# A second feed-forward worked in pairs of steps over two blocks, with split weights shared by both, rank-2 additions in four row groups, and a2 sums on VectorE

## The reference

```python
def qlora(x, wq, A, B):                 # wq is a quarter as wide as x
    return x @ tile(wq, (1, 4)).T + (x @ A.T @ B.T) * 0.5
gate = silu(qlora(x, w1q, a1, b1))      # x: 2048 x 1024, hidden: 2752
up = qlora(x, w3q, a3, b3)
y = qlora(gate * up, w2q, a2, b2)       # a2: 2 x 2752, b2: 1024 x 2
out = layernorm(x + y)
```

## Time and profile before

| | |
|---|---|
| median of 3 runs (2038.76 to 2041.78) | 2039.27 us |
| the profiled execution: its own time, its span | 2040.68 us, 2038.9 us |
| busy over the span: PE, DVE, ACT, POOL | 1999.7, 1109.3, 798.6, 1085.7 us |
| chain that ended last | PE 73%, POOL 8%, issue 8%, DVE 5%, ACT 4%, DMA 1% |
| subtractions h2l (L577), 128x512 and 112x512 | 88, 121.9 us, mean 1386 ns |
| subtractions w13l (L489) | 96, 123.5 us, mean 1291 ns |
| products h (L1198) | 88, 60.8 us, mean 691 ns |

### The profile page before, as it was taken

The page is one execution under the profiler, slowest core; times in us unless marked ns, Lnnn a source line. Parts: engine busy times, 40 slices in busy tenths (PEclk is TensorE's granted clock), DMA queues, the critical chain, the costliest instruction groups (busy, mean ns, idle before and its releaser), DMA issues.

```text
span 2038.9 us, 26001 instructions
## 1 busy us (share of the span) xinstructions
PE 1999.7 (98%) x9472; PEld 1636.0 (80%) x9472; DVE 1109.3 (54%) x1650; ACT 798.6 (39%) x1336; POOL 1085.7 (53%) x828
## 2 busy tenths in 40 slices
PE   8999999999999999999999999999979999999998
PEld 6887878888888888888888888888857777777776
DVE  0148975689863248976432888650145353454543
ACT  3356434562333347232333742422425325153251
POOL 6446874445546444644644455445738447175381
PEclk9999999999999999999999999999989999999999
DMA  4333433233434332443433243334422405124031
GB/s 139 96 92 94 130 92 88 86 132 99 135 87 127 98 94 93 136 133 93 124 98 93 89 139 99 129 100 149 142 73 93 144 21 175 42 92 145 21 134 42
DMA packets 104173, 213.40 MB, mean 105 GB/s; under 512 B 11896, under 2 KB 18040, under 8 KB 103012
## 3 DMA queue, kind: packets, MB, share of 16 engines
q1 hardware_dynamic: 99440, 194.97, 31.1%
q10 hardware_dynamic: 4608, 16.78, 2.1%
HBM read 194.93 MB, written 16.78 MB: 104 GB/s over the span
## 4 chain that ended last, share of the span: by engine, by line
PE 73%; issue 8%; POOL 8%; DVE 5%; ACT 4%; DMA 1%; SPq 0%; POOLq 0%; DVEq 0%; ACTq 0%
PE bank L1278 23%; PE bank L1279 23%; PE bank L1280 23%; POOL w13l L489 3%; POOL h2l L577 3%; ACT junka L669 2%; PE bank L1316 2%; POOL wl L489 1%; DMA w_in_place<-in_wd 1%; PE bank L1471 1%; PE bank L1433 1%; POOL xTl L489 1%; DVE scr L961 1%; ACT wh L620 1%; POOL hql L583 1%
## 5 line engine op out<-in xcount | busy, mean ns | idle before, releaser
L489 POOL TENSOR_TENSOR wl<-w_in_place,wh 128x512 fp32r<-128x512 f32 (+2 forms) x528 | 711.1, 1350 | 663.2 <-ACT wh L620 662.7
L620 ACT CAST wh<-w_in_place 128x512 fp32r<-128x512 f32 (+2 forms) x528 | 322.4, 613 | 768.3 <-DMA w_in_place<-in_wu 287.0
L1278 PE MATMUL bank<-wh,xTh 128*128 128x512 f32 (+1 forms) x1536 | 571.9, 372 | 12.1 <-POOL wl L489 11.7
L1280 PE MATMUL bank<-wh,xTl 128*128 128x512 f32 (+1 forms) x1536 | 569.4, 371 | 0.0
L1279 PE MATMUL bank<-wl,xTh 128*128 128x512 f32 (+1 forms) x1536 | 569.3, 371 | 0.0
L1278 PEld LDWEIGHTS bank<-wh,xTh 128*128 128x128 f32 x1536 | 290.1, 189 | 63.8 <-issue 8.5
L1280 PEld LDWEIGHTS bank<-wh,xTl 128*128 128x128 f32 x1536 | 290.0, 189 | 50.4
L1279 PEld LDWEIGHTS bank<-wl,xTh 128*128 128x128 f32 x1536 | 290.1, 189 | 49.5
L1278 PE MATMUL bank<-wh,hTh 128*128 128x512 f32 (+1 forms) x704 | 274.6, 390 | 1.5 <-POOL wl L489 1.2
L1279 PE MATMUL bank<-wl,hTh 128*128 128x512 f32 (+1 forms) x704 | 274.1, 389 | 0.0
L1280 PE MATMUL bank<-wh,hTl 128*128 128x512 f32 (+1 forms) x704 | 273.9, 389 | 0.0
(11 more groups left out here) (132 smaller groups left out, 2463.2 us busy)
## 6 DMA issues: line engine op xcount, KB each, us to landing
w_in_place<-in_wg SPq DMA_DIRECT2D x160, 256.0 KB, 2.6
w_in_place<-in_wu SPq DMA_DIRECT2D x160, 256.0 KB, 2.6
w_in_place<-in_wd SPq DMA_DIRECT2D x160, 256.0 KB, 2.6
w_in_place<-in_w SPq DMA_DIRECT2D x90, 256.0 KB, 3.8
x_in_place<-in_xT SPq DMA_DIRECT2D x32, 256.0 KB, 3.6
y<-in_xtok SPq DMA_DIRECT2D x4, 2048.0 KB, 8.9
x<-y ACTq DMA_DIRECT2D x16, 512.0 KB, 4.2
xa<-x SPq DMA_DIRECT2D x16, 512.0 KB, 5.5
```

Source lines behind the costliest of these rows:

```text
L489: nc.gpsimd.tensor_tensor(lo, landed, hi.bitcast(F32), ALU.subtract).then_inc(done, 1)
L620: nc.scalar.copy(hi, piece).then_inc(hi_done, 1)
L1278: nc.tensor.matmul(dst, ah, bh, start=start, stop=False)
L1280: return nc.tensor.matmul(dst, al, bh, start=False, stop=stop)
```

## The change

The second feed-forward is worked in two halves of two blocks. Within a half, the order is by pairs p of steps (11), and for each pair both blocks bb:

- w13 comes in pieces that hold two steps, two a pair (gate, up), and is loaded, cast and subtracted once per pair and half, for both blocks. The ring is two pairs deep.
- Gate and up of both steps use four banks, and alternating pairs all eight. The four rank additions follow the 24 matmuls with w13, each on 6 rows that start at partition 0, 32, 64 or 96. For this b13, a13s and the low-rank x (`lx`) hold the three parts of the split at six rows in each row group; a13s is 102 columns wide. `low_rank_x` is three passes over 102 rows.
- The products with a2 leave TensorE: VectorE multiplies each h2 by the two a2 columns and adds (`acc`), four operations a pair. At the end of a block the sum is split (`split_sums`) and added over the partitions by four matmuls with a matrix of ones in chosen columns, `sel` (`low_rank_h`), placed after the first 18 matmuls of the output stage. h2 is not split any more.
- x of blocks 0 and 1 is turned and folded ahead of the first half; that of blocks 2 and 3 in the output stages of blocks 0 and 1. x1T has two slots.
- The norm of a block now follows its output stage tile by tile. The fills for the split (`split_b`, `split_x`, `sel`) are made by GpSimd at piece 4 of the last down stage, one after another, and b1, b3, b2 are loaded by 18 DMAs at piece 9.

```diff
+UP = 32
+QUAD = (0, UP, 2 * UP, 3 * UP)
+LX = QUAD[-1] + 3 * R
+PAIRS = STEPS // 2
...
 # sync
-                if d == 23:
+                if d == 9:
                     load_b()
...
+            def load_13(h, p):
+                n = PAIRS * h + p
+                if n >= 2:
+                    sp.wait_ge(w13_used, n - 1)
...
 # gpsimd, at piece 4
+                    nc.gpsimd.memset(braw[:, :], 0.0).then_inc(b_zero, 1)
+                    nc.gpsimd.memset(b2raw[0:LR, :], 0.0).then_inc(b_zero, 1)
+                    for part, new, old, n in ((split_b, (LORA, -1.0), (0.0, 1.0), 2 * R), (split_x, (1.0, -1.0), (0.0, 1.0), R)):
+                        for i in range(2):
+                            fill(part[:, i:i + 1], old[i])
+                            for p0 in QUAD:
+                                fill(part[p0:p0 + n + R, i:i + 1], new[i])
+                                fill(part[p0:p0 + n, i:i + 1], old[i])
...
+            def pairs(h):
+                for p in range(PAIRS):
+                    if p < PAIRS - 1:
+                        low_13(h, p + 1)
...
+                    for bb in range(2):
+                        if ends(p):
+                            low_q(h, p // 2, bb)
...
 # scalar
+                        for i in range(2):
+                            act.wait_ge(gg_done, 2 * s + i + 1)
+                            if s:
+                                act.wait_ge(h_done, 2 * s + i - 1)
+                            nc.scalar.activation(sg[0:rows, i, :], banks[4 * (s % 2) + 2 * i][0:rows, :], ACT.Silu)\
+                                .then_inc(s_done, 1)
...
 # vector
+            def pair(h, p, bb):
...
+                for i in range(2):
+                    dve.wait_ge(uu_done, 2 * s + i + 1)
+                    dve.wait_ge(s_done, 2 * s + i + 1)
+                    V.tensor_tensor(h2[0:rows, i, :], banks[4 * (s % 2) + 2 * i + 1][0:rows, :], sg[0:rows, i, :], ALU.mult)\
+                        .then_inc(h_done, 1)
+                dve.wait_ge(h_done, 2 * s + 2)
+                total = fold[bb][0:rows, c, :]
+                if p % 2 == 0:
+                    ins = V.tensor_tensor(total, h2[0:rows, 0, :], h2[0:rows, 1, :], ALU.add)
+                else:
+                    step(V.tensor_tensor(total, total, h2[0:rows, 0, :], ALU.add))
+                    st.done()
+                    ins = V.tensor_tensor(total, total, h2[0:rows, 1, :], ALU.add)
...
+                for i in range(2):
+                    for r in range(R):
+                        w, part = a2raw[0:rows, 2 * p + i, r:r + 1], acc[0:rows, bb, r, :]
+                        if p == i == 0:
+                            step(V.tensor_scalar(part, h2[0:rows, i, :], w, None, ALU.mult))
+                        else:
+                            step(V.scalar_tensor_tensor(out=part, in0=h2[0:rows, i, :], scalar=w, in1=part,
+                                                        op0=ALU.mult, op1=ALU.add))
+                    st.done()
...
+            def second(b):
+
+                if b % 2:
+                    split_sums(b)
                 low_rank_h(b)
+                last = b == NB - 1
                 for t in range(NT):
...
+                        if t == NT - 1:
+                            low_rank_x(b + 2)
                     take_out(b, t)
...
 # tensor
-            def low_h(b, m, frees):
...
+            def pair(h, p, bb):
...
+                xh, xl = xsh[:, bb, :, :], xsl[:, bb, :, :]
+                for i in range(2):
+                    for w in range(2):
+                        dst = banks[4 * (s % 2) + 2 * i + w][0:rows, :]
+                        if p:
+                            pe.wait_ge((s_done, h_done)[w], 2 * (s - 2) + i + 1)
                             pe.sem_inc(passed_pe, 1)
...
+                    for w, done in enumerate((gg_done, uu_done)):
+                        p0 = QUAD[2 * i + w]
+                        nc.tensor.matmul(banks[4 * (s % 2) + 2 * i + w][0:rows, :], b13[p0:p0 + 3 * R, mm],
+                                         lx[p0:p0 + 3 * R, bb, :], start=False, stop=True).then_inc(done, 1)
+
+            def low_rank_h(b):
+
+                pe.wait_ge(acc_ready, b + 1)
...
+                for r in range(R):
+                    nc.tensor.matmul(banks[4][0:LR, :], sel[:, r, :], acch[:, r, :], start=r == 0, stop=False)
+                    ins = nc.tensor.matmul(banks[4][0:LR, :], sel[:, r, :], accl[:, b % 2, r, :], start=False, stop=r == R - 1)
+                ins.then_inc(t2_done, 1)
```

More of the change, by code:

```diff
@@ L268, in program @@
+        assert over["at"] <= at["junkd"]
+        over["at"] = at["sgn"]
         sg = put("sg", [P, 2, TB], F32)
         h2 = put("h2", [P, 2, TB], F32)
[L270 to L277, removed]
@@ L865, in _ @@
                 for t in tiles:
[L866 to L867 removed]
+                    norm_out(NB - 1, t)
         @block.vector
@@ L1240, in _, with pairs @@
-            for t in range(NT):
-                fold_x(0, t)
-            low_rank_x(0)
-            def block_2(b):
-                steps_2(b)
+            def pairs(h):
+                for p in range(PAIRS):
+                    for bb in range(2):
+                        pair(h, p, bb)
+                        if p == PAIRS - 1 and bb == 0:
+                            split_sums(2 * h)
+                        s = number(0, p, bb)
+                        if h == 0 and 1 <= s <= NT:
+                            norm_sums(NB - 1, lambda t: y[:, t, :], [s - 1])
+                        if h == 0 and s == 7:
+                            norm_bias(NB - 1)
@@ L1269, in _ @@
-            norm_bias(2 * NB, BACK)
+                    dve.wait_ge(e_evac, 2 * NT * b + 2 * (t + 1))
+                    n = NB + b + (last and t == NT - 1)
+                    norm_sums(n, lambda t: y_tile(b, t), [t], slice(0, NT) if not last else FRONT if t < NT - 1 else BACK)
+                    if last and t == NT - 2:
+                        norm_bias(n, FRONT)
+                norm_bias(NB + b + last, BACK if last else slice(0, NT))
+            for b in range(2):
+                for t in range(NT):
+                    fold_x(b, t)
+                low_rank_x(b)
@@ L1272, in _ @@
+            for h in range(2):
+                pairs(h)
+                second(2 * h)
+                second(2 * h + 1)
         @block.tensor
@@ L1564 @@
     w13 = np.stack([by_step(np.asarray(w).reshape(I, KQ, P)) for w in (L0_ffn_w1q, L0_ffn_w3q)])
-    w13 = np.ascontiguousarray(w13.transpose(1, 0, 3, 4, 2))
+    w13 = w13.transpose(1, 0, 3, 4, 2)
+    pieces = np.zeros((PAIRS, 2, P, KQ, 2, P), w13.dtype)
+    for m in range(STEPS):
+        c, q, rows = place(m)
+        pieces[m // 2, :, :, :, m % 2, :rows] = w13[c, :, :, :, q * rows:(q + 1) * rows].transpose(0, 2, 1, 3)
     def low_b(b):
```

698 lines of the change are left out of this document (353 added, 345 removed).

## The result

The changed kernel takes 1994.81 us (median of 4 runs, 1992.02 to 1995.52), the kernel before 2040.46 on the same chip: ratio 0.9774 (0.9757 to 0.9791), faster by 45.6 us, more than twice the 20 us predicted. The profiled execution took 1995.52 us, its span is 1993.7.

A forecast was written before the change was run, and what follows sets the result against it. VectorE was taken as the new bound, at 6.9 us per pair. Pair stages -31.9, between halves +3.0, output stages +9.5, edges -1 and +1 sum to -19.4 from 2039.3: about 2019 us, range 1988 to 2040.

The forecast's parts named there:

- The pair of 6.9 us on VectorE: Pair stages: VectorE needs 5.4 us clean plus 1.5 for GpSimd subtractions, 6.9 us per pair, against 6.0 for TensorE.
- The price of 1.0: Pair stages: each GpSimd subtraction costs VectorE about 1.0 us, at 1.5 subtractions per pair.
- The bound of 5.9: Pair stages: lower bound of VectorE's time per pair in us, with a third of the price per subtraction.
- Who bounds: Pair stages: VectorE is the new bound, over 90% busy; TensorE, at 85 to 88%, waits for its h products.
- rival (a): Pair stages: VectorE not the bound, subtractions find its gaps; pairs at 6.0, 1975 us, or 1998 with VectorE at 6.4; chance 0.22.
- The row groups "worth nothing in themselves": Pair stages: side-by-side rank additions gain nothing in themselves, since TensorE waits for VectorE's h_done instead.
- The additions at 0.5 us: Pair stages, TensorE: four rank additions taken at 0.5 us per pair, between 0.23 side by side and 0.92 one after another.
- rival (c): Pair stages: rank additions cost 1.7 us, TensorE at 7.24 binds again, 2034 us; chance 0.13 together with the full lock.
- The a2 products: Pair stages, TensorE: four a2 matmuls gone, 0.92 us per pair, 40.6 us over 44 pairs.
- The output stages: Output stages: +9.5 us in all, from -11.7 for transposes and a13 products, +3.6 for sel matmuls and stalls of 17.6.
- rival (d): Output-stage stalls: clock falls to 1.2 GHz, 2.7 us each, up to 11; chance 0.10 for several stalls with it or rival (b).
- The edges: Ahead of the first pair -1 us (-3 to +4); fills, loads and an extra VectorE pass earlier +1 (0 to +5).

The follow-up runs named there:

- run 3: The changed kernel with only the last of the four rank additions of each pair: 1994.83 us.
- run 4: The changed kernel with the four rank additions taken over all 102 rows instead of 6 rows in four row groups: 1995.02 us.
- run 12: The changed kernel with VectorE's output-stage order changed as in order 9, and the four rank additions over all 102 rows: 1979.30 us.
- run 5: The changed kernel with VectorE's a2 sums done only for each block's first pair of steps: 1982.33 us.
- run 6: The changed kernel with w13l written by ScalarE as a second copy, not by GpSimd's subtraction: 1979.16 us.
- order 9: The changed kernel with second-block a2 sums split right behind the first block's rank-4 values, and the last tile's output ahead of the low-rank input: 1978.05 us.
- run 2: The changed kernel with all four rank additions of a pair in the first row group: 2009.29 us.

## Why the prediction was wrong, by its own steps

**The pair of 6.9 us on VectorE is the term that failed.** Its parts: 5.4 clean (measured 5.29), and 1.5 subtractions at 1.0 us. The price of 1.0 is right for a subtraction that runs wholly beside folds and sums (0.90 to 1.06). The step that failed is the sentence that puts all of them there ("their triggers ... fall in the time of the sums"): 26 of 64 run beside folds and sums for less than half their time, 19 of these mostly beside the products from PSUM, which the prediction itself had called exempt. So they cost 0.66 on average in the changed kernel, 0.63 where 44 were taken away and 0.78 where 40 were added, and a pair takes 6.27 us and not 6.9. The bound of 5.9 was made with a third of the price, so the measured one lay inside. By VectorE's own starts (h, 1529.07 to 1662.66 in half 0, 8.0 for block 3's norm taken off, and 1778.92 to 1904.10 in half 1) twenty pairs take 125.6 and 125.2 us instead of 138.0: 25.2 less. The stages came out only 19.6 shorter: half 0's first h is 2.5 us earlier than predicted (TensorE starts at 0.23 us intervals there, not at 0.43), half 1's 1.7 later (its first pair takes 7.68 us, behind the wait of 3.3 us at the border and partly at 1.2 GHz), and TensorE's last pair now ends each stage, 2.9 and 3.6 us behind the point where VectorE frees the banks. Where the subtractions fall moves with everything else: with TensorE a little faster (run 3) more of them meet the sums, and VectorE's pair grows to 6.48 us.

**Who bounds was right, in a way that the page hides.** VectorE sets the pair stages: runs 3, 4 and 12 move TensorE's pair between 6.11 and 6.39 us without effect, and runs 5 and 6 shorten VectorE's and gain. But no wait for h shows it. TensorE's waits name GpSimd's w13l, or the split of the sums a stage later. The nearest case on record is rival (a) in its form with VectorE at 6.4 us, 1998; I gave it a small chance because VectorE would have to lose so little to a subtraction. Its reason, that the subtractions find VectorE's gaps and products, is what came in part. Its main form, TensorE alone at 6.0, is what run 6 built: 6.13 us and 1979, where 1975 stood.

**The row groups "worth nothing in themselves"** held: 11 us on TensorE, 0 in the total. The additions at 0.5 us were 0.65, with rival (c) at 1.7 off. The Trainium skill ("TensorEngine Tiling (Array Packing)", key properties) has a drain at each change of tiling mode; the trace agrees in that a group has 0.4 us of edges, two together.

**The a2 products** I counted at 40.6 us; left out of the kernel before, with the casts, subtractions and waits that hang on them, they are worth 45.6.

**The output stages**, predicted at +9.5, came out at -0.3 us. The stalls of blocks 1 and 3 are there (4.8 and 3.0 foretold, 4.5 and 2.5 found), those of blocks 0 and 2 (3.9, 3.9, 2.0) are absent: VectorE, at 6.3 us a pair, ends the sums of pair 20 at about 1667.5, 0.6 us after TensorE's border (1666.93), and their split is done before the 18 matmuls ahead of the sel matmuls are. Wider a13s weights cost nothing, as said (16 matmuls in 1.91 us before and after). The clock, rival (d), which I left out, took 2.2 us in block 1 and 1.8 in block 3.

**The edges**: +3.0 at the first pair for 0. TensorE's wait of 2.8 us for wl in the down stage, where the kernel before has 1.2 us in all, is the start of it, and a stretch at 1.2 GHz follows it (starts 0.43 to 0.53 us apart from 1388.83 on); +3.0 was in the range given there. How much of it is the fills and how much SyncE's loads stays open.

## What to carry to other kernels

An engine with slack in buffers can be the bound with no wait in its name: compare its own pace per unit of work (starts of one line) with that of the engine that is thought to bind, and look for its debt at the end of the stage. Slow that engine's rival down by a few per cent on purpose: if the time stays, the gain there is not to be had. A price read from two instructions side by side holds for those that are side by side: count how many will be, instead of charging it to all. And where a large saving (the a2 products) comes with several small ones, time the large one alone first. Here it was as large as the whole gain, and what the small ones are worth has to be asked with the moved work in place, which no run here did.

## What the runs showed of the hardware that was not expected

- Four 6-row matmuls of 512 columns in four row groups take the time of one within 0.02 us, but a group of them between 128-row matmuls costs 0.4 us at its edges; 102-row and 96-row ones cost none (0.23 us each in the stream).
- VectorE's operations on two SBUF inputs lost 0.90 to 1.06 us to a GpSimd subtraction that ran wholly beside them, and the subtraction grew from 1.30 to some 1.75 us. VectorE's products with one input in PSUM kept their 0.69 us, and a subtraction beside them its 1.30. Over whole stages the average loss was 0.63 to 0.78 us a subtraction, by how many fell where.
- Behind a stall of TensorE of 4.5 us inside a dense stage the granted clock was 1.2 GHz for a few microseconds, which cost 2.2 us. The 2.5 us stall of block 3 cost 1.8 us so (its first tile 13.89 us against 9.62 with order 9), but the same stall in runs 2 and 5 had no lower clock behind it (12.29 us).
